# Two of eight probability blocks per batch turned by 16-bit DMA transposes instead of TensorE, with the output products in another order

## What is computed

```python
qkv = jnp.einsum('bse,he->bsh', x, w_qkv)          # x is already layer-normed
q, k, v = jnp.split(qkv, 3, axis=-1)
scores = jnp.einsum('bqh,bkh->bqk', q, k) * scale
probs = jax.nn.softmax(scores, axis=-1)            # per batch 1024 x 1024
out = jnp.einsum('bqk,bkh->bqh', probs, v)
out = jnp.swapaxes(out, 1, 2).reshape(Bn, Sn, H)
out = jnp.einsum('bsh,eh->bse', out, w_proj) + b_proj
```

## Time and profile before

| | |
|---|---|
| median of 3 runs | 1958.07 us (1957.98 to 1960.77) |
| the profiled execution | 1962.98 us |
| its span, first to last instruction | 1961.0 us |
| PE, DVE, ACT, POOL busy | 98%, 70%, 53%, 27% |
| first logits of round 4 to those of round 5 | 305.63 to 374.66 us |
| last output product of the attention starts | 561.28 us |
| mean granted clock of TensorE | 0.997 |

### The profile page before, as it was taken

One profiled execution on the slowest core, in us unless ns is written; L12 is line 12 of the kernel. 1 busy time (PEld: TensorE's weight loads), 2 busy tenths in 40 slices (PEclk: granted clock), 3 DMA queues, 4 the chain that ended last, 5 costly groups with the idle time before them and its releaser, 6 DMA issues.

```text
span 1961.0 us, 29127 instructions
## 1 busy us (share of the span) xinstructions
PE 1931.2 (98%) x10638; PEld 1655.8 (84%) x10638; DVE 1363.9 (70%) x2602; ACT 1036.3 (53%) x1929; POOL 522.5 (27%) x626
## 2 busy tenths in 40 slices
PE   8999999999999999999999999999999999999996
PEld 6888888888888888888888888888888888888886
DVE  6777787777776778667677766657565656666647
ACT  5456576666755334445455454545454555445455
POOL 0031132123120001232432332343234323332246
PEclk9999999999999999999999999999999999999999
DMA  3113323334243111433434434343435344434566
GB/s 130 54 33 109 76 99 108 98 96 119 66 163 131 66 65 42 134 77 100 94 85 106 90 94 87 90 104 90 106 91 104 86 109 93 101 83 103 155 217 172
DMA packets 153338, 197.38 MB, mean 101 GB/s; under 512 B 104448, under 2 KB 121088, under 8 KB 145152
## 3 DMA queue, kind: packets, MB, share of 16 engines
q1 hardware_dynamic: 127824, 158.00, 25.7%
q0 software_dynamic: 25392, 37.77, 12.0%
HBM read 114.38 MB, written 59.34 MB: 89 GB/s over the span
## 4 chain that ended last, share of the span: by engine, by line
PE 64%; DVE 4%; another core or an unknown queue 1%; ACT 1%; issue 0%; DVEq 0%; POOL 0%; ACTq 0%; POOLq 0%
PE mo_psD L1630 12%; PE mo_psG L60 7%; PE mo_psU L62 7%; PE mo_psU L60 7%; PE mo_psG L61 7%; PE mo_psG L62 7%; PE mo_psU L61 7%; PE mo_psD L1635 6%; PE mo_psD L60 1%; PE mo_psD L61 1%; PE mo_psD L62 1%; DVE mo_HF L1979 1%; PE mo_psX L1355 1%; DVE mo_H_lo L1889 0%
## 5 line engine op out<-in xcount | busy, mean ns | idle before, releaser
L1767 ACT ACTIVATE mo_HF<-mo_psG 128x512 f32<-128x512 f32 x320 | 191.7, 599 | 388.4 <-PE mo_psU L62 312.8
L2273 POOL DMA_INDIRECT ACC<-OUT,mo_GI x128 | 201.8, 1577 | 632.5 <-DVE OUT L2062 621.0
L1979 DVE TENSOR_TENSOR mo_HF<-mo_psU,mo_HF 128x512 f32<-128x512 f32 x320 | 220.1, 688 | 202.0 <-ACT mo_HF L1767 192.0
L60 PE MATMUL mo_psG<-mo_XT_hi,wg_hi 128*128 128x512 f32 x640 | 254.6, 398 | 2.2 <-DVE mo_HF L1979 2.1
L1630 PE MATMUL mo_psD<-wd,mo_H_hi 128*128 128x512 f32 x1024 | 256.3, 392 | 0.3 <-DVE OUT L2062 0.3
L60 PE MATMUL mo_psU<-mo_XT_hi,wu_hi 128*128 128x512 f32 x640 | 250.0, 391 | 0.0
L61 PE MATMUL mo_psG<-mo_XT_lo,wg_hi 128*128 128x512 f32 x640 | 249.9, 390 | 0.0
L62 PE MATMUL mo_psG<-mo_XT_hi,wg_lo 128*128 128x512 f32 x640 | 249.4, 390 | 0.0
L61 PE MATMUL mo_psU<-mo_XT_lo,wu_hi 128*128 128x512 f32 x640 | 249.1, 389 | 0.0
L62 PE MATMUL mo_psU<-mo_XT_hi,wu_lo 128*128 128x512 f32 x640 | 249.0, 389 | 0.0
L1630 PEld LDWEIGHTS mo_psD<-wd,mo_H_hi 128*128 128x128 f32 x1024 | 185.7, 188 | 35.2 <-DVE OUT L2062 0.5
(11 more groups left out here) (354 smaller groups left out, 3996.2 us busy)
## 6 DMA issues: line engine op xcount, KB each, us to landing
X1a<-wg_in SPq DMA_DIRECT2D x16, 1024.0 KB, 4.9
X1a<-wu_in SPq DMA_DIRECT2D x16, 1024.0 KB, 4.8
X1a<-wd_in SPq DMA_DIRECT2D x16, 1024.0 KB, 4.8
XN<-XG SPq DMA_DIRECT2D x8, 1088.0 KB, 4.2
X<-x_in SPq DMA_DIRECT2D x8, 1024.0 KB, 5.3
out_dram<-X SPq DMA_DIRECT2D x8, 1024.0 KB, 6.4
XN2T<-xn2T SPq DMA_DIRECT2D x8, 1024.0 KB, 5.1
X1a<-xt_in SPq DMA_DIRECT2D x7, 1024.0 KB
```

The source lines that it names most:

```text
L60: pe.matmul(out, w_hi, x_hi, start=first, stop=False)
L1767: a.activation(HF[:, it % 2, :], psG[:, it % 2, :], ACT.Gelu).then_inc(s_gelu, 1)
L1979: v.tensor_tensor(HF[:, it % 2, :], psU[:, it % 2, :], HF[:, it % 2, :], ALU.mult).then_inc(s_mul, 1)
L2273: g.indirect_dma_start(out=io["ACC"], out_offset=bass.IndirectOffsetOnAxis(ap=GI[n % 2][:, 4 * tb + t:4 * tb + t + 1], axis=0), in_=OUT[:, ...
```

## The change

Blocks 3 and 5 (`BY_DMA`) of each batch are no longer turned by PE. ACT splits their probabilities into low and high 16-bit halves (`p_halves`, behind the exponential), SP issues two transposing DMAs per block (`turn_p`), DVE joins the turned halves in PJ (`join_p`), which lies on the memory of PT_lo, ACT copies the high part from PJ (`p_hi`), and DVE writes the low part (`p_lo`). One buffer for halves and one for turned halves serve both blocks, so each waits for the one before. The output products follow `ORDER` at the steps in `OUT_STEP`: blocks 0, 1, 2, 4, 3, 6, 5, 7 at steps 2, 3, 4, 6, 7, 8, 9, 9; step 5 has none and step 9 two. An output's sum and O parts follow in the step behind. The joins of the layer-norm output move to steps 0 to 2. Two semaphores are merged into others, and the load of XR0, whose memory now holds the halves, waits for the last subtraction.

```diff
+        PJ = nc.alloc_sbuf_tensor_at("PJ", [P, 2, S], F32, offset=nc.sbuf_base - 4 * 2 * S)
...
+        BY_DMA, BY_PE = (3, 5), (0, 1, 2, 4, 6, 7)
+        NQ, NE = len(BY_DMA), len(BY_PE)
+        ORDER, OUT_STEP = (0, 1, 2, 4, 3, 6, 5, 7), (2, 3, 4, 6, 7, 8, 9, 9)
+        half_words = c.XR0[:, :, :].rearrange("p k t -> p (k t)").bitcast(U16).rearrange("p (z n) -> p z n", z=2)
+        p_turned = xn2T[:, 1, :].bitcast(U16).rearrange("p (z n) -> p z n", z=2)
+        def joined(n):
+            return PJ[:, n % 2, :].rearrange("p (t c) -> p t c", t=NT)
+        def joined_words(n):
+            return PJ[:, n % 2, :].bitcast(U16).rearrange("p (n z) -> p z n", z=2)
+        def turned_in_front(i):
+            return max(ORDER.index(j) + 1 for j in BY_PE if j < i) if i else 0
+        def outputs_at(step):
+            return [n for n in range(NT) if OUT_STEP[n] == step]
@@ SP @@
+            def turn_p(r, i):
+                wait(sp, s_ph, by_dma(r, i) + 1)
+                wait(sp, s_ptl, joined_in_front(r, i))
+                sp.sem_inc(c.s_pass, 1)
+                for z in range(2):
+                    sp.dma_start(out=p_turned[:, z, :].rearrange("p (m t) -> p m t", t=P), in_=half_words[:, z, :],
+                                 transpose=True).then_inc(s_tr2, 16)
...
                     sp.dma_start(io["XN2T"][r - 2], xn2T[:, :, :]).then_inc(s_xtst, 16)
+                if R.gate:
+                    wait(sp, s_xtst, 16 * (r - 1))
+                turn_p(r, 3)
                 if R.ln_next:
                     sp.dma_start(xT, io["xt"][r + 1]).then_inc(s_xs, 16)
...
+                turn_p(r, 5)
+                if R.ln_next:
                     wait(sp, s_xs, 48 * r + 32)
                     sp.dma_start(rsb[:, :], io["RS"][r + 1].partition_broadcast(P)).then_inc(s_xs, 16)
...
+            sp.wait_ge(s_ptl, 16 * NB)
             sp.dma_start(c.XR0[:, :, :], io["XN2T"][0][:, :, 0:512]).then_inc(c.s_xr0, 16)
@@ PE, behind S(step) @@
-                    if 0 <= i1 < NT:
-                        turn_p()
-                    if i2 >= 0:
-                        output(range(NT))
+                    if i1 in BY_PE:
                         wait(pe, s_exp, 8 * r + i1 + 1)
+                        wait(pe, s_ptl, 2 * (8 * r + turned_in_front(i1)))
...
+                    for n in outputs_at(step):
+                        wait(pe, s_os, 8 * r + n - 1)
...
+                        wait(pe, s_pth, 2 * (8 * r + n + 1))
...
+                        wait(pe, s_ptl, 2 * (8 * r + n + 1))
@@ ACT @@
+            def p_halves(R, i):
+                wait(a, s_exp, 8 * r + i + 1)
+                wait(a, s_tr2, landed(r, R.gate, BY_DMA.index(i)))
+                for z in range(2):
+                    j = a.activation(half_words[:, z, :], Pr[:, i % 2, :].bitcast(U16).rearrange("p (n z) -> p z n", z=2)[:, z, :],
+                                     ACT.Copy)
+                j.then_inc(s_ph, 1)
+            def p_hi(r, i):
+                n = ORDER.index(i)
+                wait(a, s_pv, 8 * r + n - 1)
+                wait(a, s_ptl, 2 * (8 * r + n) + 1)
+                a.activation(PT[0][:, n % 2, :, :], joined(n), ACT.Copy).then_inc(s_pth, 2)
...
+                    if step == NT:
+                        p_hi(r, i3)
+                    if i1 in BY_PE:
...
+                    if i3 in BY_DMA and step < NT:
+                        p_hi(r, i3)
+                    if i0 in BY_DMA:
+                        p_halves(R, i0)
+                    if R.gate and step < 3:
+                        join(r, (((0, 0),), ((1, 0),), ((0, 1), (1, 1)))[step])
@@ DVE: the maximum is taken under i0 < NT, the reciprocal behind p_lo at NT, the psPT subtractions under BY_PE @@
+                    for n in outputs_at(step - 1):
+                        sum_output(n)
                     if i0 < NT:
...
+                    if i3 in BY_DMA:
+                        join_p(i3)
                     if R.ln_next and step == NT + 1:
                         scaled_lo(r + 1, (2, 3))
+                    for n in outputs_at(step - 1):
+                        output_lo(n)
+                    if step == NT:
+                        p_lo(i3)
...
+                    if i1 in BY_PE:
...
+                    if i3 in BY_DMA and step < NT:
+                        p_lo(i3)
                     if R.ln_next and step == NT:
                         scale_next(1)
                         scaled_lo(r + 1, (0, 1))
```

More of the change, by code:

```diff
@@ L424, in body @@
                 for step in range(NT + 2):
-                    i0, i1, i2 = step, step - 1, step - 2
+                    i0, i1 = step, step - 1
                     if i0 < NT:
@@ L444, in turn_p @@
                                 i.then_inc(s_t, 1)
[L446 to L453, removed]
+                    for n in outputs_at(step):
+                        wait(pe, s_os, 8 * r + n - 1)
+                        if n == 0:
+                            wait(pe, s_vl, 4 * (r + 1))
+                        wait(pe, s_pth, 2 * (8 * r + n + 1))
+                        for t in range(NT):
+                            pe.matmul(output_bank(n)[:, :], PT[0][:, n % 2, t, :], V_both[:, t, :, :].rearrange("p z d -> p (z d)"),
                                       start=(t == 0), stop=False)
[L455 to L458, removed]
+                        wait(pe, s_ptl, 2 * (8 * r + n + 1))
+                        for t in range(NT):
+                            i = pe.matmul(output_bank(n)[:, 0:D], PT[1][:, n % 2, t, :], V[0][:, t, :], start=False, stop=(t == NT - 1))
                         i.then_inc(s_pv, 1)
-                    if 0 <= i1 < NT:
-                        turn_p()
-                    if i2 >= 0:
-                        output(range(NT))
             rounds(pe, body)
@@ L482, in scaled_hi, with join @@
                     a.activation(xnT[0][:, dk, ht * 512:(ht + 1) * 512], xT[:, dk, ht * 512:(ht + 1) * 512], ACT.Copy).then_inc(s_xh, 1)
-            def join(r, z):
-                wait(a, s_tr2, 32 * (r - 1))
-                for k in range(KD):
+            def join(r, parts):
+                wait(a, s_tr2, landed(r, True, 0))
+                for k, z in parts:
                     i = a.activation(words[:, z, k, :], turned[:, z, k * S:(k + 1) * S], ACT.Copy)
-                if z == 1:
-                    i.then_inc(s_n2, 1)
+                    if (k, z) == (1, 1):
+                        i.then_inc(s_n2, 1)
+            def p_halves(R, i):
+                r = R.r
+                wait(a, s_exp, 8 * r + i + 1)
[9 more added lines that the diff above has]
+                a.activation(PT[0][:, n % 2, :, :], joined(n), ACT.Copy).then_inc(s_pth, 2)
             def norm_y(r, h):
@@ L552, in body @@
                         wait(a, s_max, 8 * r + i0 + 1)
[L553 removed]
+                        rp, ip = read_tiles(r, i0)
+                        if ip in BY_PE:
+                            wait(a, s_t, 2 * (by_pe(rp, ip) + 1))
+                        else:
+                            wait(a, s_ph, by_dma(rp, ip) + 1)
                         b = logit_bank(i0)
@@ L702, in body, with join_p, p_lo, sum_output @@
                     i0, i1, i3 = step, step - 1, step - 3
-                    if i3 >= 0:
-                        wait(v, s_pv, 8 * r + i3 + 1)
-                        v.tensor_reduce(Osum[:, i3 % 2, :], output_bank(i3)[:, :].rearrange("p (z d) -> p d z", z=2), AX.X,
-                                        ALU.add).then_inc(s_os, 1)
+                    def join_p(i):
+                        n = ORDER.index(i)
+                        wait(v, s_pv, 8 * r + n - 1)
+                        wait(v, s_tr2, landed(r, R.gate, BY_DMA.index(i) + 1))
+                        for z in range(2):
+                            j = v.tensor_copy(joined_words(n)[:, z, :], p_turned[:, z, :])
+                        j.then_inc(s_ptl, 1)
+                    def p_lo(i):
+                        n = ORDER.index(i)
+                        wait(v, s_pth, 2 * (8 * r + n + 1))
+                        v.tensor_tensor(PT[1][:, n % 2, :, :], joined(n),
+                                        PT[0][:, n % 2, :, :].bitcast(F32), ALU.subtract).then_inc(s_ptl, 1)
+                    def sum_output(n):
+                        if n == NT - 1:
+                            wait(v, s_ol, 8 * r + n - 1)
+                        wait(v, s_pv, 8 * r + n + 1)
+                        v.tensor_reduce(Osum[:, n % 2, :], output_bank(n)[:, :].rearrange("p (z d) -> p d z", z=2), AX.X,
+                                        ALU.add).then_inc(s_os, 1)
+                    def output_lo(n):
+                        i = ORDER[n]
+                        wait(v, s_oh, 8 * r + n + 1)
+                        v.scalar_tensor_tensor(O[1][:, i, :], Osum[:, n % 2, :], rinv[:, i:i + 1], O[0][:, i, :].bitcast(F32),
+                                               ALU.mult, ALU.subtract).then_inc(s_ol, 1)
```

(2 more changed lines are left out.)

51 lines of the change are left out of this document (30 added, 21 removed).

## The result

| | before | after |
|---|---|---|
| median, same chip | 1959.32 us of 4 runs (1957.98 to 1960.77) | 2006.67 us of 4 runs (2004.81 to 2009.09) |
| ratio, 95% interval | | 1.0245 (1.0233 to 1.0257) |
| the profiled execution, its span | 1962.98, 1961.0 us | 2004.81, 2003.0 us |
| mean granted clock of TensorE | 0.997 | 0.987 |

The change makes the kernel 47 us slower; 1985 (1968 to 2002) was forecast. The direction held and the time lies 4.7 us above the range.

What follows compares the result with a forecast made beforehand. TensorE, busy 98%, was taken to bound the kernel. Seven rounds losing 3.8 us each plus 0.5 in round 7 make 27.1; 1962.98 + 27.1 = 1990.1, less 4.9 for the median: 1985 us, range 1968 to 2002.

Steps and rivals of the forecast that it cites:

- DVE's queue: VectorE's in-order work in steps 5 to 9 makes TensorE wait 5.4 us a round against 1.6 spared.
- The walk: Time-by-time count through VectorE's in-order work of a round, from maximum 5 at 28.01 to output 5's sum at 52.48.
- sum(5): VectorE's reduction that frees output 5's bank; behind step 8's work it ends at 52.48, so output 7 starts at 52.6.
- DVE scales with it at 42.6: Step 8: VectorE scales the next batch with rsb, issued at up to 39.4; no wait for it was counted.
- (3): Rival: DMAs late, rsb or block 5 1 to 2.5 us behind VectorE; 1992 to 2002 us; 16%.
- Rival (4): TensorE's clock falls to 1.2 GHz in the idle before output 7, 2.8 us in seven rounds; 2005 us; 9%.
- the queue's case: Main case: VectorE's work ahead of output 5's sum sets the loss; 1985 us, own range 1977 to 1992; 60%.
- The 4.9 us: Median of the runs shown lies this far below the profiled 1962.98 us; subtracted from 1990.1 to give 1985.
- 12.6 us of spared transposes: turn(3) and turn(5) removed from TensorE, 1.58 us a round over eight rounds, won only if TensorE needn't wait.
- spare 16 us: VectorE's idle time in a 69.03 us round, 53.03 busy; said to be uneven, with a solid queue behind step 8.

Runs made afterwards that it cites:

- e10_queue: The changed kernel with rsb loaded before block 5's transposes, ScalarE's first three X1 normalizations moved later, and unused matmuls in TensorE's waits before turn(7) and output 7: 1989.74 us.
- e1_sum5: The changed kernel with the sum of output 5 taken ahead of the next batch's scaling and subtraction instead of behind them: 1981.38 us.
- e9_rsbnorm: The changed kernel with rsb loaded before block 5's transposes and ScalarE's first three X1 normalizations moved later, output 5's sum left in place: 2005.49 us.
- the square: Changed kernel, rsb late: 2006.67 us, 1999.31 with unused matmuls holding the clock; rsb early and normalizations moved: 2005.49, 1989.74 with the matmuls.
- e8_all: The changed kernel with output 5's sum early, rsb early, X1 normalizations moved later, and two pieces of VectorE work moved into its waits: 1969.33 us.
- e2_rsb: The changed kernel with rsb loaded ahead of block 5's transposes instead of behind them: 2005.88 us.
- e4_both: The changed kernel with output 5's sum ahead of the next batch's scalings and rsb loaded ahead of block 5's transposes: 1987.7 us.

## Why the prediction fell short

**DVE's queue: right.** The walk gave 3.8 us a round and 27.1 in all. With rsb and the clock taken out, e10_queue's rounds are 72.86 us against 69.03, and its last output product starts at 590.43, 29.15 us behind that of the kernel before (561.28). 2.07 of these are the idle products of round 7; 27.1 remain. In the changed kernel PE's waits, their places and their releasers were as predicted, and e1_sum5 shows that sum(5) behind the scalings makes the larger of the two, 17.2 us.

**"DVE scales with it at 42.6": the step that failed first.** The prediction had rsb's issue at up to 39.4 and set no landing against it, so the sum has this wait at nothing. The issue is at 39.0 and the landing 4.7 us later, at 43.8; DVE waits 8.5 us in all. The lateness stood in the rivals as (3), a case of 16%, where the numbers at hand made it the likelier one: the shortest landing shown was 4.3 us, and 39.4 and 4.3 are 43.7. Alone, with the clock held, it costs 9.6 us.

**The clock: the second.** The sum had it at nothing too. Rival (4) had it at 9%, on rows in which PE stood idle for 2.2 us and the clock stayed at 1.00. Here PE waits 2.0 us and, 11 us later, 2.4 us, and the clock falls in seven of eight rounds. Output 7 is slow in four of them, and by 1.5 us, not 2.8: 7.4 us in the changed kernel, 15.8 in e9_rsbnorm (2005.49 less 1989.74), some 2 us more each without the idle products of round 7. The 20 us of the rival, from output 7 alone, are near the second number by luck. Part of the cost came by a way the prediction didn't have: output 5 is slow, and it holds the PT buffer that block 7 needs.

**Rivals that were not rivals.** (3) and (4) were priced as other ways to go, each from 1985 us. They came together and on top of the queue: 2006.67 less 1989.74 is 16.9 us, and by the square they overlap. The forecast of 1985 us lacked 21.7; the other 4.7 are the next point.

**The 4.9 us, and a near hit that is luck.** The sum was turned from the profiled execution to the median by the excess of one profiled run, 1962.98 over 1958.07. That was right: the excess belongs to that run, and those of the changed kernel and of e10_queue lie 1.9 and 0.3 us below their medians. So 1985 is what the queue's case has to be held against, and e10_queue's 1989.74 is 4.7 us above it, though within the case's own range (1977 to 1992). That its profiled 1989.42 is so near the 1990.1 on the way to the sum is luck. Of the 4.7 us, 2.07 are the idle products of round 7 and 0.8 is the kernel before itself (1958.87 beside this run); some 2 us were traced to no place.

**Where the 12.6 us of spared transposes went.** DVE pays for them. Of its spare 16 us, the last stretch of the round before had only 3 (windows view of the kernel before, 17.1 us ahead of the next batch's first product):

```profile
340.14:357.23 17.09, 17.09 (x103) 15.03 (x103) 14.10 (x32) 11.87 (x23) 3.51 (x9) 1.00 0.27 92
```

Both blocks' joins, waits for p_hi and lower halves fall there, a net 2.5 us of work and 2.5 us of waiting. e8_all, with these waits made smaller by the moves that were tried, has rounds of 70.03 us, 1.0 over before, and DVE busy for 19.5 of 20.4 us at its end.

## What to carry to other kernels

Work that is taken from the bound engine and given to another is worth what that engine has free in that stretch, not in the round; here DVE was 77% busy over the round and all but full in its last 20 us. When a transfer moves in a queue, put its landing beside the moment it is wanted, not its issue. And when two waits can each cost something, price them together: they overlap, as the slow output 5 did with the wait for block 5, or one feeds the other, as a stall of 2 us of TensorE did by slowing what came after it. A filler put into a wait costs its own time where the wait is absent, 2.07 us here.

## What the runs showed of the hardware that was not expected

- GpSimd's instructions of 128x8 elements took 1.35 to 1.39 us instead of 0.20 to 0.24 in rounds 1 to 6 of e2_rsb and e4_both, where they ran beside DVE's work on operands that all lie in SBUF (a 128x512 float32 product of two tensors, a 16-bit copy); beside a subtraction that reads PSUM they kept 0.20. A wait of DVE can be what lets GpSimd through.
- The granted clock fell to 0.50 behind waits of PE of 1.9 to 2.5 us, in a kernel whose PE is busy 97% of the time; eight 128x512 products then took up to 3.7 us instead of 2.1. It didn't fall behind each such wait: 2.51 us before output 7 of round 4 left it at 1.00.
- Two 16-bit copies into every second half-word took 1.37 us where one dense 32-bit copy of as many bytes took 0.68.
- The transposes of one block (two of 128x1024 16-bit) landed 3.2 us behind their issue in the median, 4.6 at most, and took 2.6 us to issue.
